# Shifted inputs in three parts, and the feed-forward's normalisation on GpSimd

## The reference

```python
def shift_tokens(t):
    a, s = jnp.split(t, 2, -1)
    s = jnp.pad(s, ((0, 0), (1, 0), (0, 0)))[:, :-1]
    return jnp.concatenate([a, s], -1)
...
def ffn_layer(x, g, bln, W1, b1, W2, b2):
    mu = x.mean(-1, keepdims=True)
    var = ((x - mu) ** 2).mean(-1, keepdims=True)
    xn = (x - mu) / jnp.sqrt(var + 1e-05) * g + bln
    hg = xn @ W1 + b1
    a, gate = jnp.split(hg, 2, -1)
    return a * jax.nn.gelu(gate, approximate=False) @ W2 + b2
for i in range(DEPTH):
    x = attn_layer(shift_tokens(x), Wqkv[i], q_scale[i], k_scale[i], Wo[i]) + x
    x = ffn_layer(shift_tokens(x), ln_g[i], ln_b[i], W1[i], b1[i], W2[i], b2[i]) + x
```

## Time and profile before

| | us |
|---|---|
| median of 3 runs | 2810.81 (2807.93 to 2812.37) |
| the profiled execution | 2807.24 |
| its span, first to last instruction | 2805.4 |
| PE busy | 2686.3 (96%) |
| DVE busy | 2592.6 (92%) |
| ACT busy | 2248.9 (80%) |
| POOL busy | 2116.8 (75%) |

### The profile page before, as it was taken

The page is one execution under the profiler, slowest core; times in us unless marked ns, Lnnn a source line. Parts: engine busy times, 40 slices in busy tenths (PEclk is TensorE's granted clock), DMA queues, the critical chain, the costliest instruction groups (busy, mean ns, idle before and its releaser), DMA issues.

```text
span 2805.4 us, 92977 instructions
## 1 busy us (share of the span) xinstructions
PE 2686.3 (96%) x36468; PEld 2051.5 (73%) x36469; DVE 2592.6 (92%) x3379; ACT 2248.9 (80%) x3785; POOL 2116.8 (75%) x1535
## 2 busy tenths in 40 slices
PE   8899978999999999999999999999999999999998
PEld 7677756777777777777777777777777777777776
DVE  7999978999999999999999999999999999989997
ACT  5899957888787887878878788887888878778786
POOL 7866658777877777788777787777787787777773
PEclk9999999999999999999999999999999999999999
DMA  1000012232233232223232232322233322222223
GB/s 59 24 2 2 2 49 70 68 80 64 68 72 73 70 78 64 69 72 74 68 74 68 72 73 69 80 65 67 67 74 73 73 66 68 67 68 62 62 67 102
DMA packets 103879, 178.41 MB, mean 64 GB/s; under 512 B 29382, under 2 KB 52740, under 8 KB 103556
## 3 DMA queue, kind: packets, MB, share of 16 engines
q1 hardware_dynamic: 103444, 175.14, 25.7%
q10 hardware_dynamic: 240, 0.66, 0.1%
HBM read 22.62 MB, written 2.10 MB: 9 GB/s over the span
## 4 chain that ended last, share of the span: by engine, by line
PE 32%; issue 15%; POOL 14%; ACT 11%; DMA 8%; DVE 4%; SPq 1%; ACTq 0%; POOLq 0%; DVEq 0%
PE pa L985 10%; DMA kT<-spare 8%; POOL spare L1748 7%; PE px L1014 5%; PE ps L1045 4%; PE pg L1104 3%; PE pg L1128 3%; PE px L1059 3%; ACT spare L1314 2%; PE pg L1119 2%; DVE ss L1532 2%; PE pg L1072 2%; POOL spare L1757 2%; POOL pr L1786 2%; POOL first_xs_lo L1734 2%
## 5 line engine op out<-in xcount | busy, mean ns | idle before, releaser
L1748 POOL TENSOR_TENSOR spare<-spare,first_qk_t 128x1024 f32<-128x1024 f32 x384 | 911.0, 2395 | 16.1 <-POOL first_xs_lo L1734 8.1
L1764 POOL TENSOR_TENSOR sm<-sm,inv 128x512 f32<-128x512 f32 x192 | 202.0, 1052 | 427.6 <-DVE sm L1570 359.4
L1548 DVE TENSOR_TENSOR first_qk_t<-pa,first_rot 128x1024 f32<-128x1024 f32 x384 | 464.4, 1210 | 3.7 <-ACT spare L1267 3.2
L1539 DVE TENSOR_TENSOR spare<-pa,first_rot 128x1024 f32<-128x1024 f32 x384 | 464.5, 1210 | 0.0
L1532 DVE TENSOR_REDUCE ss<-spare 128x16 f32<-128x1024 f32 x384 | 457.2, 1191 | 4.4 <-ACT spare L1260 2.2
L1757 POOL TENSOR_TENSOR spare<-spare,inv 128x1024 f32<-128x1024 f32 x192 | 366.2, 1907 | 73.1 <-ACT inv L1299 67.1
L1014 PE MATMUL px<-ident_sb,spare 128*128 128x128 f32 x3072 | 408.8, 276 | 12.7 <-POOL spare L1757 6.2
L1014 PEld LDWEIGHTS px<-ident_sb,spare 128*128 128x128 f32 x3072 | 341.3, 141 | 101.3 <-issue 47.2
L1610 DVE TENSOR_TENSOR oT_lo<-px,oT_hi 128x1024 fp32r<-128x1024 f32 x192 | 226.6, 1180 | 79.7 <-ACT oT_hi L1337 79.6
L1045 PEld LDWEIGHTS ps<-kT,qT 128*32 128x32 f32 x12288 | 181.9, 110 | 128.7 <-DMA kT<-spare 64.8
L985 PE MATMUL pa<-first_w_hi,first_xs_hi 128*128 128x512 f32 x576 | 255.6, 444 | 19.4 <-DVE first_qk_t L1548 7.3
(11 more groups left out here) (218 smaller groups left out, 6570.5 us busy)
## 6 DMA issues: line engine op xcount, KB each, us to landing
kT<-spare SPq DMA_DIRECT2D x384, 256.0 KB, 3.7
pT<-prT SPq DMA_DIRECT2D x766, 64.0 KB, 2.0
w_part<-in_Wqkv SPq DMA_DIRECT2D x40, 192.0 KB, 3.7
wo<-in_Wo SPq DMA_DIRECT2D x6, 512.0 KB, 5.4
wo<-in_W SPq DMA_DIRECT2D x6, 341.0 KB, 4.6
c_h<-in_x SPq DMA_DIRECT2D x3, 512.0 KB, 6.4
spare<-in_Wqkv SPq DMA_DIRECT2D x1, 1536.0 KB, 6.7
spare<-in_x SPq DMA_DIRECT2D x4, 256.0 KB, 4.0
```

Source lines behind the costliest of these rows:

```text
L1539: dve.tensor_tensor(heads(qk_r[:, c, :]), heads(pa[(3 * j + c) % 2][:]), per_head(rot[:, l % 2, 2 * c, :]), ALU.mult).then_inc(s[cos], 1)
L1548: dve.tensor_tensor(halves(qk_t[:, c, :]), halves(pa[(3 * j + c) % 2][:])[:, :, ::-1, :], table.unsqueeze(1).to_broadcast([P, HEADS, 2, DH ...
L1748: pool.tensor_tensor(qk_r[:, c, :], qk_r[:, c, :], qk_t[:, c, :], ALU.add)\
```

## The change

`xs_hi` and `xs_lo` are filled in three parts of 256, 128 and 128 tokens. ACT makes the first two parts of the next group at j=2 (behind copy_kT) and j=3 (ahead of copy_kT), and the third part at j=2 of the group's own turn. POOL makes the first part at j=3 as before, the second at j=0, the third at the head of j=2. `project_q` now waits at j = 0, 2 and 3. ACT writes the inverse deviation to `fx` in SBUF instead of `pg`; in the group loop POOL multiplies `fc` by it, in place, between its two rotations of j=0, and norm_probs of j=0 stands ahead of the second rotation. `round_normed` and `rest_of_normed` read `fc`. In the drain DVE still multiplies.

```diff
+        SHIFT = (slice(0, 2 * P), slice(2 * P, 3 * P), slice(3 * P, 4 * P))
+        SHIFT_END = (2, 3, 4)
...
 # project_q (PE)
-                        if j % 2 == 0:
-                            pe.wait_ge(s["xs_ready"], 4 * i + j + 2)
+                        if j != 1:
+                            pe.wait_ge(s["xs_ready"], 6 * i + 2 * max(j, 1))
...
 # shift_hi (ACT)
-                        wait_for(act, s["v_full"], g * GT - 2 * (1 - half))
+                        wait_for(act, s["v_full"], (g - 1) * GT + SHIFT_END[part])
...
 # copy_centred (ACT)
-                        wait_for(act, s["fn_mul"], full_before(g))
+                        wait_for(act, s["fn_lo_ready"], full_before(g))
...
-                        act.activation(pg[:, cols(g)], fx[:, cols(g)], ACT.Exp, scale=-0.5).then_inc(s["frs_ready"], 1)
+                        act.activation(fx[:, cols(g)], fx[:, cols(g)], ACT.Exp, scale=-0.5).then_inc(s["frs_ready"], 1)
...
-                        act.activation(fn_hi[:, cols(g)], pg[:, cols(g)], ACT.Identity, bias=ln_par[:, 1:2]).then_inc(s["fn_hi_ready"], 1)
+                        act.activation(fn_hi[:, cols(g)], fc[:, cols(g)], ACT.Identity, bias=ln_par[:, 1:2]).then_inc(s["fn_hi_ready"], 1)
...
 # body (ACT)
                         copy_qT(i, j, 1)
-                        if j == 0:
-                            shift_hi(i, 0, 1)
                         if j == 2:
-                            shift_hi(i, -1, 0)
+                            shift_hi(i, 0, 2)
                         if j == 1:
                             gate_gelu(i, 2, 1)
                         square_k(i, j, 0)
+                        if j == 3:
+                            shift_hi(i, -1, 1)
                         copy_kT(i, j, 1)
+                        if j == 2:
+                            shift_hi(i, -1, 0)
...
 # normalise, rest_of_normed (DVE)
-                        dve.tensor_tensor(pg[:, cols(g)], fc[:, cols(g)], pg[:, cols(g)], ALU.mult).then_inc(s["fn_mul"], 1)
+                        dve.tensor_tensor(fc[:, cols(g)], fc[:, cols(g)], fx[:, cols(g)], ALU.mult).then_inc(s["fn_mul"], 1)
...
-                        dve.scalar_tensor_tensor(fn_lo[:, cols(g)], pg[:, cols(g)], ln_par[:, 1:2],
+                        dve.scalar_tensor_tensor(fn_lo[:, cols(g)], fc[:, cols(g)], ln_par[:, 1:2],
                                                  fn_hi[:, cols(g)].bitcast(F32), ALU.add, ALU.subtract)\
...
 # body (DVE)
-                        if j == 0:
-                            normalise(i, 2)
...
 # POOL
+                def normalise(i, back):
+                    g, live = group(i, back)
+                    if live:
+                        pool.wait_ge(s["fc_ready"], g + 1)
+                        pool.wait_ge(s["frs_ready"], g + 1)
+                        pool.tensor_tensor(fc[:], fc[:], fx[:], ALU.mult).then_inc(s["fn_mul"], 1)
...
 # body (POOL)
+                        if j == 2:
+                            shift_lo(i, 0, 2)
                         norm_scores(i, j, 2)
                         if j == 3:
                             shift_lo(i, -1, 0)
                         rotate(i, j, 0, 0, "cos_q", "sin_q", "rot_q")
+                        if j == 0:
+                            normalise(i, 2)
+                            norm_probs(i, j, 2)
                         rotate(i, j, 0, 1, "cos_k", "sin_k", "rot_k")
-                        norm_probs(i, j, 2)
+                        if j > 0:
+                            norm_probs(i, j, 2)
                         norm_keys(i, j, 0)
                         if j == 0:
                             shift_lo(i, 0, 1)
```

More of the change, by code:

```diff
@@ L1354, in tables, with shift_hi @@
                         act.preload_act_table_set(name)
-                def shift_hi(i, back, half, first=False):
+                def shift_hi(i, back, part, first=False):
                     g, live = group(i, back)
@@ L1359, in shift_hi @@
                     if live:
-                        at = bass.ds((g % GROUPS) * GTOK + half * HALF_TOK, HALF_TOK)
-                        to = slice(half * HALF_TOK, (half + 1) * HALF_TOK)
+                        to = SHIFT[part]
+                        at = bass.ds((g % GROUPS) * GTOK + to.start, to.stop - to.start)
                         act.wait_ge(s["res_ready"], g + 1)
-                        wait_for(act, s["v_full"], g * GT - 2 * (1 - half))
+                        wait_for(act, s["v_full"], (g - 1) * GT + SHIFT_END[part])
                         act.copy(xs_hi[0:64, to], res[0:64, at]).then_inc(s["xs_hi_ready"], 1)
@@ L1474, in _ @@
                 act.wait_ge(s["xs_zeroed"], 2)
-                shift_hi(0, 0, 0, True)
-                shift_hi(0, 0, 1, True)
+                for part in range(3):
+                    shift_hi(0, 0, part, True)
                 def drain():
@@ L1726, in _, with shift_lo @@
             def _(pool):
-                def shift_lo(i, back, half, first=False):
+                def shift_lo(i, back, part, first=False):
                     g, live = group(i, back)
@@ L1730, in shift_lo @@
                     if live:
-                        at = bass.ds((g % GROUPS) * GTOK + half * HALF_TOK, HALF_TOK)
-                        to = slice(half * HALF_TOK, (half + 1) * HALF_TOK)
-                        chunk = 2 * g + half
+                        to = SHIFT[part]
+                        at = bass.ds((g % GROUPS) * GTOK + to.start, to.stop - to.start)
+                        chunk = 3 * g + part
                         rest = lambda dst, src: pool.tensor_tensor(dst, src, hi, ALU.subtract)
@@ L1817, in _ @@
                 pool.wait_ge(s["xs_zeroed"], 2)
-                shift_lo(0, 0, 0, True)
-                shift_lo(0, 0, 1, True)
+                for part in range(3):
+                    shift_lo(0, 0, part, True)
                 pool.wait_ge(s["zeroed"], 7)
```

## The result

The changed kernel takes 2838.7 us (median of 4 runs, 2834.8 to 2839.8), the kernel before 2809.4 in the same session (4 runs, 2806.1 to 2812.4): a ratio of 1.0106 [1.0094, 1.0118], 1.1% slower. The forecast was 2851 with a range of 2820 to 2900. Sign and range held; the size was +30 where +40 was forecast. The profiled execution took 2837.64 us with a span of 2835.8, so 30.4 more span than before.

What follows compares the result with a forecast made beforehand. No engine alone bounds it; what can change a turn is the stretch from j=0's scores to T, through path G and path K. 36 turns x 1.01 (36.4 us) plus 3.9 in looser turns: +40.3, hence 2851; range 2820 to 2900.

Steps and rivals of the forecast that it cites:

- Path G: At j=0: DVE's maximum to subtraction, then POOL through norm_keys, which releases T; 1.00 us slack, forecast to grow 1.94.
- T: Point where PE starts the key transposes of j=1, 16.29 us after the scores of j=0; forecast 1.01 later.
- path K: From j=0: ACT's queue (shift copies, square_k, copy_kT), the kT transfer, then the scores of j=1; forecast 0.4 us shorter.
- the hold: rest_of_normed, reading two SBUF tensors on DVE, delays POOL's second rotation at j=0: 0.6 us on path G.
- looser turns: Ten of 46 turns with 1.24 to 3.71 us of slack on path G; forecast to pay 3.9 us together.
- Normalisation 1.29 us: POOL's 128x512 product between the rotations of j=0, on path G, interpolated between widths at 1.29 us.
- self-wait 0.19: On POOL at j=0, norm_keys right behind the rotation whose result it reads starts 0.19 us late.
- The earlier kT, 0.4: Without shift copies at j=0, copy_kT and the kT transfer come 0.4 us earlier; lost because PE waits at T.
- PE's own time behind T: From T to the next scores of j=0, PE runs matmuls one behind the other, about 33 us.
- Rival 2: DVE misses the gap: rest_of_normed asks after norm_probs and waits out the second rotation; +89 us, 2900; chance 0.09.
- Rival 1: rest_of_normed does not hold POOL; only 0.41 us per tight turn and 0.4 in the looser, 2826; chance 0.2.
- Rival 3: Path K decides: T up to 0.4 us earlier if path G grows under 1.00 us; 2792; chance 0.09.

Runs made afterwards that it cites:

- Experiment 1: Changed kernel, but rest_of_normed takes its first operand from PSUM bank pg instead of fc in SBUF (result wrong, same instruction shape): 2805.9 us, 0.9994.
- experiment 6: Experiment 2's kernel with only the operands and result of DVE's normalisation and rest_of_normed moved to SBUF, no new POOL work: 2824.6 us, 1.0057.
- experiment 2: Changed kernel with all normalisation edits undone (on DVE, in PSUM), leaving only the shift in three parts: 2802.6 us, 0.9981.
- experiment 5: Kernel before, plus an unread POOL product between the rotations at j=0, norm_probs ahead of the second: 2823.3 us (512 columns), 2821.8 (256, narrow).
- experiment 4: Changed kernel with the shift put back into two halves, leaving only the normalisation on POOL with SBUF operands: 2882.9 us, 1.0265.

## Why the prediction was right, and where its sizes were off

- **Path G's slack, and what spends it.** The step held. T went from clear of norm_keys' end to waiting on it (40 waits in the window above, where before has 3), and path K stopped deciding. Experiment 1 shows the other side: without the hold T is 0.27 later than before and the median turn 0.18 longer, 8 us in 45 turns, and the looser turns pay that back.
- **Normalisation 1.29 us, hold 0.6, self-wait 0.19.** Measured 1.28, 0.52, 0.08. The width interpolation was exact. The hold came from differences at 256 columns and was 0.08 high; the self-wait was read off two shift subtractions of 0.64 and was 0.11 high: behind a rotation of 2.92, norm_keys started 0.08 late. These two make T +0.80 instead of +1.01, which over 45 turns is 9 us; the median turn itself grew by 0.70.
- **The earlier kT, 0.4.** It was 0.32, and in a typical turn lost, as stated.
- **The ten looser turns, +3.9.** Here the step failed: the forecast charged them by their slack, and took for granted that a turn which was long would stay long. It did not: they came out at -4.4, so the term is off by 8.3 us and has the wrong sign.
- **PE's own time behind T, about 33 us.** It held in a typical turn (33.20 before, 33.13 after), but in all it shrank by 7.4 us, mostly waits for kT that the turn read for the forecast did not have.
- **Rival 2, the missed gap, 0.09.** It happened in 5 of 46 turns, for 10 us. I had treated it as all or none, with a margin of 0.25 us against the end of norm_probs. The margin was 0.14 against that end and 0.09 against the start of the rotation, since DVE came 0.88 behind the end of the normalisation (ACT began 0.12 behind it, took 0.73, and DVE 0.03 more) where I had 0.77. One miss came as the rival has it, by a late ACT; the four others came with DVE's row 0.07 to 0.09 ahead, inside a margin that the forecast took as safe.
- **Rival 1, no hold: 2826.** Its premise is refuted by experiments 1 and 6. Its size was off too: without the hold the kernel takes 2805.9, since the looser turns give time back.
- **Rival 3, faster if path K decides: 2792.** Path G grew by more than its slack even without the hold (T 0.27 later in experiment 1), so its condition was not met. Its gain is doubtful as well: experiment 2 has path G as before and kT earlier, and gains 5 us, not 18, because the path through DVE's queue, which I had not drawn, ends 0.07 us ahead of the old T. I had read "what ends the wait" at PE's two stops and not what stands next behind them. Experiment 2 still has the normalisation on DVE; no run has a clear path G without it.
- **The sum.** Forecast were +40.3: 36.4 in the tight turns, 3.9 in the looser. Measured are +18.8 in the tight turns without a miss, +14.0 in those with one, -4.4 in the looser and some +2 at head and tail: the 30.4 by which the span grew. That the sum came as near as a quarter is in part luck: without the 10 us of the misses, which were a rival and no part of the sum, it would have been off by half.

The Trainium skill's page SBUF — State Buffer (Who interferes with whom) goes further than the one that the prediction named: a VectorE instruction with two SBUF inputs contends with a GpSimd instruction that reads SBUF, the ports that they share are an exclusive lock, and the order of issue decides who is blocked. The traces agree that each can block the other: POOL is held for 0.43 to 0.52 us in the one order, DVE for 2.23 (2.98 - 0.75) in the other. On the order itself they agree only roughly: in four misses DVE's row begins first, by 0.07 to 0.09 us, and DVE is the one that waits.

## What to carry to other kernels

Count the SBUF operands of every VectorE instruction that runs beside a busy GpSimd, before moving a tensor from PSUM to SBUF: here one such operand in one instruction of 0.75 us cost about 30 us over 46 turns, and the work moved onto GpSimd about 3. Where the two engines' starts fall within a tenth of a us of each other, price both orders and expect a mixture, since in the dearer order VectorE waited for the whole of a GpSimd instruction of 2.4 us. Before charging the turns that were already long, ask what made them long, and whether the changed kernel still has it: here they gave 4.4 us back. And before promising a gain from a shorter path, ask which path is next: here it was 0.07 us behind.

## What the runs showed of the hardware that was not expected

After the 2.03 us in which PE stood still for fn_lo, the granted clock fell. Busy time by stretch, around the missed turn of 724.11; the third column from the right is the granted clock:

```profile
739.20:740.40 1.20, 1.11 (x4) 0.98 (x5) 1.20 (x4) 0.10 (x1) 1.20 (x1) 0.87 0.00 0
740.40:742.40 2.00, 2.00 (x6) 1.52 (x5) 2.00 (x3) 1.49 (x2) 1.43 (x3) 0.50 0.18 41
742.40:743.70 1.30, 1.30 (x4) 0.95 (x4) 1.30 (x2) 0.00 (x0) 0.00 (x0) 0.57 0.46 106
743.70:745.00 1.30, 1.30 (x11) 1.03 (x10) 0.71 (x2) 1.06 (x2) 0.45 (x1) 1.00 0.15 33
```

0.50 is the 1.2 GHz level. The matmuls of 128x512 then follow each other every 0.43 us (740.49 to 740.92 above) instead of 0.24 (739.62 to 739.86), until the clock is back at 1.00. It happened in three of the five misses, where PE had stood for 1.99 to 2.03 us, and T came at 19.2 to 19.6 there; in the two others PE stood for almost as long (1.95 and 1.98 us), the clock stayed at 1.00, and T came at 18.0.

The kernel before has it too, behind two waits for kT of 2.08 and 2.04 us at the scores of j=1. PE's timeline and the busy time behind the first of them:

```profile
1973.27 1.03 PE L1045 MATMUL ps<-kT,qT 128*32 128x64 f32 x29 [2.08 <-DMA kT<-spare]
```

```profile
1973.27:1976.60 3.33, 3.33 (x71) 3.16 (x72) 1.83 (x4) 1.81 (x3) 3.25 (x3) 0.50 0.00 0
```

These are its two longest turns, 52.3 and 52.5 us; in the changed kernel the waits at that place are at most 1.43 us, the clock stays up, and the two turns take 50.0 and 50.2. That is part of what the looser turns gave back. The length of the wait alone does not decide: in experiment 5 with the narrow product PE stood for 2.17 us and the clock stayed at 1.00. In experiment 4 the misses left PE idle for 1.6 us and the clock did not fall behind them, which fits that a miss cost less there than forecast.

A POOL product also depends on its operands, not on its width alone: 128x512 takes 1.28 us from two full tensors, 1.04 when both inputs are the same tensor (experiment 5), and 1.05 with a broadcast one.
